# A vision-tower layer on one core: mix, both norms, attention and routing in one pipeline over image pairs

## The reference

```python
h = tok(x, ...)                           # patches with shifted copies and a wavelet branch, layer norm, matmul
h = h + attn(_layernorm(h), ...)          # windows of 3 tokens at 4 scales, gelu, one 192x192 matmul (owT)
xn = _layernorm(h)                        # the norm of the whole block, without weights
xn1 = _layernorm(xn, norm1_w, norm1_b)
qkv = xn1 @ qkv_w.T + qkv_b               # 12 heads of 16, 49 tokens of one image
o = softmax(q @ k.T * scale) @ v
x2 = xn + (o @ proj_w.T + proj_b)
xn2 = _layernorm(x2, norm2_w, norm2_b)
logits = xn2 @ w_gate                     # 8 experts, the best 2 of each token, softmax of the two
x2 + sum over experts of gate * (gelu(xn2 @ W1 + b1) @ W2 + b2)
```

## Time and profile before

| what | us |
|---|---|
| median of 3 runs | 1294.85 (1292.99 to 1303.62) |
| profiled execution, its own time | 1294.28 |
| its span in the trace | 1292.4 |

### The profile page before, as it was taken

How to read it: one execution, slowest core, us unless ns; L and a number is a source line. 1 busy time by engine, 2 the same in 40 slices (tenths; PEclk the granted TensorE clock), 3 DMA queues, 4 the chain that set the end, 5 groups by cost and what they waited for, 6 DMA issues and landing times.

```text
span 1292.4 us, 25004 instructions
## 1 busy us (share of the span) xinstructions
PE 1074.6 (83%) x7254; PEld 951.0 (74%) x7255; DVE 714.4 (55%) x1825; ACT 432.1 (33%) x1092; POOL 559.3 (43%) x1075
## 2 busy tenths in 40 slices
PE   7899899899899788763888888989737999999930
PEld 4799899899898556462777677767626999999930
DVE  6566466366354888752677878787651222222224
ACT  0321222212211233331555555455302444444422
POOL 0555455455442344211356666666541444444410
PEclk9888888898898899775999989899757999999975
DMA  9545047056100200025600000000011111111114
GB/s 341 198 173 233 9 197 276 24 200 245 55 8 10 75 0 0 25 50 176 247 11 15 14 14 14 14 19 14 15 43 31 43 44 43 37 43 43 43 67 160
DMA packets 48120, 105.54 MB, mean 82 GB/s; under 512 B 6827, under 2 KB 36117, under 8 KB 45266
## 3 DMA queue, kind: packets, MB, share of 16 engines
q1 hardware_dynamic: 38242, 92.65, 19.8%
q0 software_dynamic: 5760, 9.68, 2.1%
...
...
## 4 chain that ended last, share of the span: by engine, by line
issue 32%; POOLq 22%; PE 15%; DVE 10%; POOL 10%; DVEq 3%; DMA 3%; SPq 2%; ACT 2%; ACTq 0%
POOLq L536 6%; PE pe L1483 5%; POOLq L1250 5%; POOLq L514 2%; DVE prod L322 2%; POOL xs_d L506 2%; POOLq L503 2%; DMA x<-yy_d 2%; DVE sc L325 1%; POOL hall L517 1%; DVEq L323 1%; POOL xn L509 1%; PE pe L1487 1%; PE pp L843 1%; DVE pv L339 1%
## 5 line engine op out<-in xcount | busy, mean ns | idle before, releaser
L1483 PE MATMUL pe<-wm,xm 128*128 128x193 f32 x1008 | 200.1, 365 | 1.7 <-DVEq L1336 1.7
L1483 PEld LDWEIGHTS pe<-wm,xm 128*128 128x128 f32 x1008 | 196.7, 219 | 2.8 <-issue 2.7
L802 ACT ACTIVATE hT<-pe,eb 128x128 f32<-128x128 f32 x336 | 93.1, 376 | 147.4 <-PE pe L911 147.4
L924 PE MATMUL pp<-w2s,hT 128*128 x672 | 118.5, 326 | 0.0
L924 PEld LDWEIGHTS pp<-w2s,hT 128*128 128x128 f32 x672 | 107.9, 190 | 0.2
L908 PE MATMUL pe<-xsT,ew 128*128 128x128 f32 x672 | 90.4, 286 | 3.5 <-ACT xsT L792 3.5
L724 DVE TENSOR_TENSOR ys<-pp,b2s 128x192 f32<-128x192 f32 x56 | 20.0, 358 | 125.6 <-PE pp L924 125.6
L532 POOL DMA_INDIRECT yy_d<-ys,yix x56 | 68.3, 1220 | 46.4 <-issue 46.4
L908 PEld LDWEIGHTS pe<-xsT,ew 128*128 128x128 f32 x672 | 81.7, 196 | 9.1 <-ACT xsT L792 4.2
L1175 ACT ACTIVATE sqt<-xm 128x2688 f32<-128x2688 f32 x14 | 34.2, 2444 | 146.1 <-DMA xm<-in_xm 42.8
L506 POOL DMA_INDIRECT xs_d<-xsrc,dst x64 | 65.5, 1023 | 40.3 <-issue 40.3
...
## 6 DMA issues: line engine op xcount, KB each, us to landing
...
xs<-xs_d SPq DMA_DIRECT2D x56, 96.5 KB, 1.9
...
```

Source lines behind the costliest of these rows:

```text
L802: last = f(self.hT[:, u, c], pe1[:, 2 * u + c % 2, (c // 2) * ROWS:(c // 2 + 1) * ROWS], ACT.Gelu, bias=self.b1[:, u, c:c + 1])
L924: last = mm(pp[:, u, 0:D], self.hT[:, u, n], self.w2s[:, bass.ds(e, 1), n * D:(n + 1) * D].rearrange("p o d -> p (o d)"), start=(n == 0), ...
L1483: mm(y[:, 0:D + 1], cell(q, c), wm[:, q, c], start=(q + c == 0), stop=(q == 3 and c == KC - 1))
```

## The change

The separate `mix` loops and the copy through `h2_d` are gone. `accT` is laid out by image pair, padded to 64 columns an image; SP copies one pair's 96x2x128 block at a time from `accT` to one of four buffers `mixT` (98 KB), and the `owT` product of the pair is the first step of the pair pipeline (`n0`), added to `hall`, which is loaded by pairs from the start. The pipeline is 14 deep instead of 8, has 45 slots, and is unrolled by four. The q and k products are done for two pairs at once in every second slot, 196 columns wide, with q and k of four heads in one 128-row product; the norm's small POOL ops, the routing and the rank run for two pairs at once. Scores are twelve matmuls of 32x64 by 98 columns in place of four of 96x64 by 294. The first norm's weight goes into the q, k, v weights and its bias into `qkb`, `bv` and the projection's bias row; the gate matmul becomes eight more columns of the value product and of the projection. These folds are computed by a new class `Folds` after the windows. The second norm's weight and bias are no longer applied by POOL; ACT applies them in the expert stretch while it copies `xsT`. The expert weights are loaded in 16 parts among the first slots, `b1s` and `b2s` ahead of them.

```diff
-        def mix(item):
-            i, u, h = item(0)
-            pe.wait_ge(self.st3_set[u % 2], 2 * h + u // 2 + 1)
-            pe.wait_ge(self.h2_set, i + 1)
-            mm(pe1[:, u, 0:D], self.st3[0:H2, u, 0], self.owT[0:H2, 0], start=True, stop=False)
-            mm(pe1[:, u, 0:D], self.st3[:, u, 1], self.owT[:, 1], start=False, stop=True).then_inc(self.mix_mm, 1)
-        run_slots(pe, TT, 1, mix, 4)
...
-        def mix(item):
-            i, u, _ = item(0)
-            dve.wait_ge(self.mix_mm, i + 5)
-            row = self.hall[:, bass.ds(i, 1), :].rearrange("p o d -> p (o d)")
-            v.tensor_tensor(row, row, self.pe1[:, u, 0:D], ALU.add).then_inc(self.h2_set, 1)
-        run_slots(dve, TT, 1, mix, 4)
+            if u == 5:
+                self.folds.gate(dve)
+            if u == 10:
+                self.folds.row(dve)
+        last.then_inc(self.acc_set, 1)
...
-        for g in range(5):
-            sp.wait_ge(self.h2_set, 5 * g + 9)
-            for q in range(2):
-                dst = self.h2_d.rearrange("b (i t) d -> t b i d", t=2)[q, :, 5 * g:5 * g + 5, :]
-                sp.dma_start(dst, self.hall[q * B:(q + 1) * B, 5 * g:5 * g + 5]).then_inc(self.s["h2_st"], 16)
-        if not heads:
-            sp.wait_ge(self.s["h2_st"], 160)
+        rows = self.base_d.rearrange("t (i q) d -> q t i d", q=2)
+        for q in range(2):
+            sp.dma_start(self.hall[q * B:q * B + T], rows[q, 0:T]).then_inc(self.s["base_ld"], 16)
+            sp.dma_start(self.hall[q * B + T:(q + 1) * B], rows[q, 0:B - T]).then_inc(self.s["base_ld"], 16)
+        heads.load_weights(sp)
...
+        mm(pe1[:, 2, 0:E], h.ones[:], h.wgp[:, 0], start=True, stop=False)
+        mm(pe1[:, 2, 0:E], h.ones[0:LOW], h.wgp[0:LOW, 1], start=False, stop=True)
+        mm(pe1[:, 2, E:2 * E], vecs[:, 9:10].to_broadcast([P, P]), h.wg2[:, 0], start=True, stop=False)
+        mm(pe1[:, 2, E:2 * E], vecs[0:LOW, 8:9].to_broadcast([LOW, P]), h.wg2[0:LOW, 1], start=False, stop=True)
+        for n in range(3):
+            bank, a, r = (3, 4, slice(0, LOW)) if n != 1 else (1, 3, slice(LOW, P))
+            mm(pe1[:, bank, n:n + 1], wM[:, n * P:(n + 1) * P], vecs[:, a:a + 1], start=True, stop=False)
+            mm(pe1[:, bank, n:n + 1], wR[r, n // 2 * P:(n // 2 + 1) * P], vecs[r, 5:6], start=False, stop=True)
+        for n in range(2):
+            mm(pe1[0:H2, 3, 3 + n:4 + n], wM[:, 3 * P + n * H2:3 * P + (n + 1) * H2], vecs[:, 4:5], start=True, stop=False)
+            last = mm(pe1[0:H2, 3, 3 + n:4 + n], wR[0:LOW, 2 * P + n * H2:2 * P + (n + 1) * H2], vecs[0:LOW, 5:6], start=False, stop=True)
+        last.then_inc(self.mm, 1)
+        pe.wait_ge(self.bias_set, 1)
...
+    def bias(self, dve):
+        h, v = self.h, self.h.nc.vector
+        dve.wait_ge(self.mm, 1)
+        v.scalar_tensor_tensor(h.wM[:, 3 * P + D:], h.pe1[:, 2, 0:E], -1 / D, h.wgp[:, 0], ALU.mult, ALU.add)
+        v.scalar_tensor_tensor(h.wR[0:LOW, 2 * P + D:], h.pe1[0:LOW, 2, 0:E], -1 / D, h.wgp[0:LOW, 1], ALU.mult, ALU.add)
+        v.tensor_copy(h.c0[:], h.pe1[:, 2, E:2 * E])
+        for n, bank in enumerate((3, 1, 3)):
+            v.tensor_tensor(h.qkb[:, n:n + 1], h.pe1[:, bank, n:n + 1], h.vecs[:, 10 + n:11 + n], ALU.add)
+        v.tensor_tensor(h.bv[:], h.pe1[0:H2, 3, 3:5], h.vecs[0:H2, 15:17], ALU.add)
+        dve.drain().then_inc(self.bias_set, 1)
+
...
+            if n13:
+                i, u, _ = n13
+                pool.wait_ge(self.dst_set, groups(n13))
+                pool.wait_ge(self.xs_set, i + 1)
+                g.tensor_copy(self.xsrc[:, u, :, D:DX], ids[:, bass.ds(i, 1), :].rearrange("p o k -> p k o"))
...
-            if b:
-                pool.wait_ge(self.c_x, b[0] + 1)
-                g.tensor_tensor(self.xn[:, b[1]], self.xn[:, b[1]], self.n2[:, 0], ALU.mult)
...
-            if b:
-                g.tensor_tensor(self.xn[:, b[1]], self.xn[:, b[1]], self.n2[:, 1], ALU.add).then_inc(self.c_xn, 1)
...
+                if u % 2 == 1:
+                    pool.wait_ge(self.mv2_set, i + 1)
+                    r2 = self.r2[:, bass.ds(i - 1, 2)]
+                    tt(r2, self.mv2[:, u - 1:u + 1, 1], eps, ALU.add)
+                    pool.drain()
+                    tt(r2, r2, mhalf, ALU.pow).then_inc(self.r2_set, 1)
+                pool.wait_ge(self.x_set, i + 1)
+                tt(row, row, self.x2[:, u], ALU.add).then_inc(self.res_set, 1)
+            if n0 and n0[1] % 2 == 1:
+                i, u, _ = n0
+                two = bass.ds(i - 1, 2)
+                var, r1, rr, q1 = self.mv[:, u - 1:u + 1, 1], self.r1[:, two], self.rr[:, two], self.q1[:, two]
+                a, w, r = (self.tmp[:, n] for n in range(3))
+                pool.wait_ge(self.mv_set, i + 1)
+                tt(a, var, eps, ALU.add)
                 pool.drain()
...
+            if n4:
+                i, u, _ = n4
+                gr = u // 2
+                dve.wait_ge(self.qk_mm, groups(n4))
+                wait(dve, self.s_mm, i - 3)
+                for n in range(3):
+                    bank, a = ((0, 0), (1, 0), (0, 4 * T))[n]
+                    last = v.scalar_tensor_tensor(self.kbd[:, gr, :, n], pt1[B:P, bank, a:a + 4 * T].unsqueeze(1).to_broadcast([B, 2, 4 * T]),
+                                                  self.qkb[B:P, n:n + 1], masks.to_broadcast([B, 2, 4 * T]), ALU.add, ALU.mult)
+                last.then_inc(self.k_set, 1)
...
-            f(self.xsT[:], pt1[:, u, 0:2 * ROWS].rearrange("p (h n) -> p h n", h=2), ACT.Copy).then_inc(self.e_xT, 1)
+            for h in range(2):
+                last = f(self.xsT[:, h], pt1[:, u, h * ROWS:(h + 1) * ROWS], ACT.Identity, bias=self.vecs[:, 8 + h:9 + h], scale=self.vecs[:, 6 + h:7 + h])
+            last.then_inc(self.e_xT, 1)
...
-                pe.wait_ge(self.a_xT, n1 + 1)
-                pe.wait_ge(self.a_v, n1)
-                pe.wait_ge(self.a_k, n1)
-                for g in range(2):
+            n0, n3, n4, n5, n6, n7, n8, n11, n12 = (item(lag) for lag in (0, 3, 4, 5, 6, 7, 8, 11, 12))
+            if n7:
+                i, u, _ = n7
+                pe.wait_ge(self.s_ex, i + 1)
+                wait(pe, self.on_set, i)
...
+            if n6:
+                i, u, _ = n6
+                a, gr = u % 2 * 2 * T, u // 2
+                wait(pe, self.s_sub, i)
+                pe.wait_ge(self.q_set, groups(n6))
+                pe.wait_ge(self.k_set, groups(n6))
+                for n in range(6):
                     for m in range(2):
-                        for h in range(2):
-                            rows = H2 + h
-                            mm(pp[0:H2, g, m * P:(m + 1) * P], self.wqk[0:rows, h, g * D + m * H2:g * D + (m + 1) * H2],
-                               self.xT2[0:rows, h], start=(h == 0), stop=(h == 1))
+                        r, c = slice(n % 2 * 32, n % 2 * 32 + 32), a + m * T
+                        last = mm(pe1[m * B:(m + 1) * B, n % 2, n // 2 * 2 * T:(n // 2 + 1) * 2 * T], self.qT[r, n // 2, gr, c:c + B],
+                                  self.kbd[r, gr, :, n // 2, c:c + T], start=True, stop=True)
+                last.then_inc(self.s_mm, 1)
...
+            if n0:
+                _, u, k = n0
+                pe.wait_ge(self.mix_ld[u], 16 * k + 16)
+                mm(pt1[:, 1, 196:196 + D], self.mixT[0:H2, u, 0], self.owT[0:H2, 0], start=True, stop=False)
+                mm(pt1[:, 1, 196:196 + D], self.mixT[:, u, 1], self.owT[:, 1], start=False, stop=True).then_inc(self.mixed, 1)
+            if n8:
+                i = n8[0]
+                pe.wait_ge(self.onT_set, i + 1)
+                mm(pp[:, 0, 256:256 + D + E], self.onT[0:H2, 0], self.wproj[0:H2, 0], start=True, stop=False)
+                mm(pp[:, 0, 256:256 + D + E], self.onT[:, 1], self.wproj[:, 1], start=False, stop=True).then_inc(self.proj_mm, 1)
...
-                mm(pt1[:, 1, 0:E], self.ones[:], self.acc[:], start=True, stop=False)
-                mm(pt1[:, 1, 0:E], const[:, C_TRI:C_TRI + P], self.ohs[:], start=False, stop=True).then_inc(self.d_rank, 1)
...
+            if n4 and n4[1] % 2 == 1:
+                i, u, _ = n4
+                pe.wait_ge(self.xT_set, i + 1)
+                if n0:
+                    pe.wait_ge(self.h2_set, n0[0] + 1)
+                x = [xT[:, h, u - 1:u + 1].rearrange("p a (m t) -> p (a m) t", t=B)[:, :, 0:T] for h in range(2)]
+                out = pt1[:, 0, 0:4 * T], pt1[:, 1, 0:4 * T], pt1[:, 0, 4 * T:8 * T]
+                low, high = slice(0, LOW), slice(LOW, P)
+                for n in range(3):
+                    mm(out[n], wM[:, n * P:(n + 1) * P], x[1 - n % 2], start=(n < 2), stop=False, skip_group_check=True)
+                for n in range(3):
+                    r = high if n == 1 else low
+                    last = mm(out[n], wR[r, n // 2 * P:(n // 2 + 1) * P], x[n % 2][r], start=False, stop=True, skip_group_check=True)
+                last.then_inc(self.qk_mm, 1)
...
```

(16 more changed lines are left out.)

816 lines of the change are left out of this document (439 added, 377 removed).

## The result

The changed kernel took 1361.8 us (median of four, 1358.8 to 1370.3) beside 1299.2 us for the kernel before (median of four, 1293.0 to 1312.0): ratio 1.048, 95% interval 1.042 to 1.054. The forecast was 1234 us, in a range of 1190 to 1275, with 0.06 for slower.

The account below looks back on a forecast made before the run. POOL was taken to bind the pair pipeline's later slots, with PE and DVE close behind. From 1294.28 us, -81.0 for start and pipeline and +20.5 for the experts gave 1234 us; 8-in-10 range 1190 to 1275.

Parts of the forecast that it names:

- the pipeline's clock: Pair pipeline: PE's granted clock stays at 0.90, full slots take 8.3 us, the whole pipeline 295 us against 360.3.
- a sign of being wrong: Pair pipeline: the forecast is wrong if the granted clock there falls under 0.8.
- the prediction's own sum, 8.6: One full pipeline slot: 7.5 us of PE work becomes 8.3 at clock 0.90, slot 8.6; 8.3 was taken.
- PE's work: One full pipeline slot: PE's products sum to 8.1 us, times 0.92 for overlap, 7.5 us busy.
- rival 1: Pair pipeline and experts: scores run side by side in 0.6 us, experts' copy hidden, 1192 us; chance 0.16.
- The cover of `on`: Pair pipeline: PE needs DVE's `on` only after the next slot's transposes and scores, giving 2.3 us of cover.
- Rival 3: Pair pipeline: PE waits more, at its lower clock for half the slots; 11.5 us a slot, 1311 us; chance 0.05.
- The start: From the windows to the first norm of the pair pipeline: it starts at 581.0 us, 15.9 us earlier.
- The experts: Expert tiles: two activations take 0.80 us where one copy took 0.42, nothing hides 0.38; +20.5 us over 54 tiles.
- `kbd`: DVE in the pair pipeline: `kbd` ops halve to 16 x 3, each about 0.6 us.
- Tail: The kernel's end: no change, 0 us.
- the gap before the experts: From the pipeline's end to the first expert load: 15.9 us, taken as unchanged.

Follow-up runs that it names:

- e6: The changed kernel plus eight products of 128 rows by 128 columns per slot, work for nothing, ahead of the values' product: 1274.2 us, ratio 0.980 to before.
- e1: The changed kernel with eleven of a pair's twelve score products reading 64 rows instead of 32 (wrong values): 1411.1 us, ratio 1.081 to before.
- e10: The changed kernel plus eight light products (32 rows by 64 columns) per slot, work for nothing: 1413.5 us, ratio 1.076 to before.
- e11: The changed kernel with half-row products zero-padded to 128 rows, four added dense products per slot, and experts' first activation releasing PE by itself: 1272.8 us, ratio 0.972 to before.
- e5: The changed kernel plus four light products (32 rows by 64 columns) per slot, work for nothing: 1311.8 us, ratio 1.010 to before.
- e4: The changed kernel with the experts' two scale-and-bias activations replaced by one 256-column copy, omitting the second norm's weight and bias: 1339.4 us, ratio 1.024 to before.

## Why the prediction was wrong

**The step that failed** is the pipeline's clock: "at the 0.90 seen, 7.5 would become 8.3". I carried the granted clock of the kernel before over to another set of products. The clock was 0.55, under the 0.8 that the prediction itself gave as a sign of being wrong, the mean slot 11.3 us for 8.3, and the pipeline, up to DVE's last work, 402.1 us for 295. 31 slots x 3.0 us are 93 of the 107 us. (The 8.3 also lay 0.3 under the prediction's own sum, 8.6, with no reason given; that is 7 us of them.) At the upper level the slot was priced well: 7.5 us (641.95 to 656.97, above) for 7.8, if by two errors that cancel, as below. With dense products the clock is back, and e6, at 0.98, has a mean slot of (885.9 - 616.0) / 31 = 8.7 us with 2.05 us of such products in it:

```profile
L686 DVE TENSOR_REDUCE mx<-pe x32: 769/770/771, 616.0 to 885.9; 128x12 f32<-128x588 f32 x32
```

**PE's work** was priced 1.0 us too dear a slot: 6.5 us at the upper level, not 7.5. Scores take 0.73 us, near the 0.6 of rival 1, whose rule of the Trainium skill (TensorEngine Tiling (Array Packing), Theoretical Speedup), up to 4x for a dimension of at most 32, this row bears out in sign: 24 instructions of 32 rows and 98 columns in 0.73 us where 24 of 128 rows and 34 columns (L1024) take 0.90. These are also the products that use least of the array; that they are what lowers the clock is not shown, since e1 did not test it.

**The cover of `on`** was misread. I wrote that PE needs `on` "only after its transposes and scores of the next slot, 2.3 us of cover". L964 itself waits for it, since both use one bank, and `kbd` stands before it on DVE. At the upper clock this costs 1.54 and 1.96 us in the slots with q and k, 1.0 us a slot where the prediction had 0.3. The clock reads 1.00 up to 667 us, 0.62 from 667 to 668 and 0.50 from there: it falls right behind the second such wait (665.07 to 667.03). After that the waits are fewer (12.2 us from 680 to 940), probably because PE is slow enough, and the clock stays down. What ends a spell at 1.00 the runs don't settle: e10 fell near 707 with no wait, and e11 still shows 19.7 us of waits for `onT` and 10.7 for `on` from 680 to 860 at 0.93.

**Rival 3** had the result, with a chance of 0.05. Its reason, more waiting, is neither shown nor ruled out for this kernel: the fall at 667 came behind a wait, but e10 stayed low with hardly any. I argued against it that PE's busy share rises. The share did rise, to 95%, and the clock was 0.55 all the same; e5 shows one busy share at both levels. The rows on record could have warned me: in the earlier trace rows PE is busy for 9.09 of 10 us at 0.50. That its 11.5 us a slot lie near the mean of 11.3 is luck: it had 7.5 us of work with half of the slots low, the runs had 6.5 with nearly all of them low (0.54 from 680 to 940). The Trainium skill (TensorE: Matmul & The Clock Gate, Part 1) lets activity release the upper clock. If activity is read as the busy share of the records, e10 does not agree: 219 of 220 us busy at 0.59.

**The start**: -11.4 for -15.9. The first product waits for `mixT`, which lands later than I priced:

```profile
583.87 0.16 DVE L641 COPY acc<-const 1x8 f32<-1x8 f32 x1
584.58 0.36 SPq L1090 DMA_DIRECT2D xs_d<-zero  x1
585.00 0.42 SPq L1093 DMA_DIRECT2D b1s<-in_b  x1
585.47 0.97 SPq L1093 DMA_DIRECT2D b2s<-in_b  x1
586.48 1.37 SPq L1101 DMA_DIRECT2D mixT<-accT  x2
...
591.61 0.98 PE L1009 MATMUL pt<-owT,mixT 96*128 96x192 f32 x2 [13.45 <-DMA mixT<-accT]
```

From the end of DVE's part to the first product it is 7.6 us, where 6.3 to the landing had been summed; `accT` itself was complete at 583.4, which is 575.2 without the 8.2 us, for 573.0. No run took `b1s` away, so what part of it is the 24-byte pieces, for which the prediction took 1 us, is open.

**The experts**: right. 0.84 us for the two activations, tile 5.01 us (gelus at 1099.97 and 1104.98) for 4.97, PE idle 0.51 us before its weight load. e4 shows the cause by taking it away: 22 us. The +23.8 of the table are 3.3 more than the +20.5.

**`kbd`**: 48 ops of 0.63 us for 0.60. **Tail** and the gap before the experts: within 2 us.
